# Where GpSimd clears tiles and splits weights in a four-block attention and expert kernel

## Chip, cores and metric

The kernel runs on one core of one Trainium2 chip. The metric is the device time of one execution in microseconds (us). The engines are TensorE (PE), VectorE (DVE), ScalarE (ACT), GpSimd (POOL) and SyncE (SP, which issues all DMAs here).

## What is computed

x has 4 images of 256 tokens of 128 values; the context has 4 images of 64 tokens. Four residual blocks follow one another:

```python
x = x + cross_attention(layernorm(x), ctx)            # 16 heads of 8, biases on q, k, v, out
x = x + moe(layernorm(x))                             # 8 experts, top 2 by sigmoid, relu squared, plus one shared
x = x + decoder(layernorm(x), ctx)                    # a: causal self-attention and norm; c: cross-attention
                                                      # and norm; f: dense, relu, norm
x = x + experts(layernorm(x))                         # top 1 of 7 by softmax, gated silu 512 wide, plus one shared
```

The result must be precise to float32, so most products are made from a high and a low half in float16 (high times high, high times low, low times high: L877 to L879). Each weight and each activation that enters such a product is first split: the high half is a cast, the low half the difference.

## The kernel before

**Work and its tiles.** The images are b = 0 to 3, in two groups g = 0 (images 0, 1) and g = 1 (images 2, 3). All the work is cut into events, each a tuple such as `("scores", a, b, u)`: attention a (0 cross-attention of the first block, 1 self-attention, 2 cross-attention of the third), image b, unit u. An attention of an image is: `nat` (the q or k product) and its `stack` (three DMAs by SP that lay the high and low halves into interleaved partitions), `kblocks` (DVE spreads the keys block-diagonally, four copies: into KBX for the context, L1431, into kbs for self-attention, L1429), `max` (PE makes scores, DVE takes the maximum of each head, L1484: 4 units, 12 in self-attention), `negmax` (the negated maxima scaled and split by DVE, L1493 and L1496, turned by PE, laid into the stacked queries by a DMA of SP), `scores` (PE, then the exponential on ACT), `pv`, `o_take`, `out_norm`, `flip` and `square` (the output product and the residual sum). `ln_stats` is DVE's mean and variance, `ln_pow` POOL's power -1/2, `ln_plain`, `ln_center` and `ln_norm` the rest of a norm. `gate0` is the first expert gate (13 small steps of DVE, L1531 to L1552), `spread` lays its weights over the partitions through the tile wpad (L1640, L1641, PE L1091), `up0` and `down0` are the experts.

**Weights.** They come in 11 pieces into the two halves of wraw (`load`, by SP). `split` (DVE, L1379) casts a piece to its high half wh; `split_low` (POOL, L849, three events a piece, 0 to 2) subtracts and writes wl. A piece may be loaded once the piece two before it has been split. Pieces 0 to 2 serve the attentions and the first experts, pieces 3 to 10 (1536 columns each) only the last block.

**Clearing.** `kbs_zero` (POOL, L827 to L831) clears kbs and VS, which self-attention needs later. KBX has been cleared at the start.

**What sets the order.** Nothing is ordered by hand. `steps()` says which event must come behind which. `parts()` gives each event its engines and their planned durations. `schedule()` is a list planner: among the events that could start soonest it takes the one with the largest urgency, which is the longest planned chain behind it, less GROUP_LEAD for group 1, plus numbers of the table PRESSING by kind, group and name. Its result is one fixed order per engine; each engine then runs its list in that order and waits on semaphores. Where the planner leaves PE idle, `keep_running` puts filling matmuls on the identity matrix (L888), as many as the planned gap asks for.

```python
def urgency(e):
    return todo[e] - GROUP_LEAD * group(e) + PRESSING.get(e[0], 0) + PRESSING.get((e[0], group(e)), 0) + ...
```

POOL's two branches that matter here, as they were:

```python
elif kind == "kbs_zero":
    for i in range(2):
        nc.gpsimd.memset(kbs[:, i].bitcast(U32), 0).then_inc(zeroed, 1)
...
elif kind == "split_low":
    _, i, j = e
    pool.wait_ge(w_high, nth[("split", i)])
```

Of the kernel before, what the change touches and what calls it, by code (L numbers as in the profile page):

```python
# [16 lines left out]
B, S, SC = 4, 256, 64  # L17
# [36 lines left out]
GROUP_LEAD = 5.7  # L54
TABLE_LOAD = 1.3
FLIGHT = {"load": 4.3, "stack": 2.0, "clear": 3.5, "negmax": 2.0, "fetch": 3.0, "slots": 3.0}
# [9 lines left out]
def steps():  # L66
# [3 lines left out]
    def chain(seq, *first):  # L70

        prev = list(first)
        for e in seq:
            after.setdefault(e, []).extend(prev)
            prev = [e]
        return prev[0]

    def also(e, *before):
        after[e].extend(before)

    bias = chain([("bias",)])
    ctx = chain([("split", 0), ("ctx",)])
    k0 = chain([("kblocks", 0, 0)], chain([("stack", "k0", 0)], chain([("nat", "k0", 0)], ctx, bias)))
    masks1 = chain([("masks1",)])
    biases = chain([("bias_split",)], ("split", 1))
    room = chain([("kbs_zero",)], *[("ln_pow", "x0", b) for b in range(B)])
    v0 = chain([("vctx", 0)], k0)
    for i in range(1, PIECES):
        if i >= 2:
            chain([("load", i)], ("split_low", i - 2, 2) if i > 2 else ("split", 0), *([("load", i - 1)] if i > 2 else []))  # L90
        chain([("split", i)], ("split", i - 1), *([v0] if i == 1 else [("load", i)]))
        chain([("split_low", i, j) for j in range(3)], ("split", i), *([("split_low", i - 1, 2)] if i > 1 else []))

    k2 = chain([("stack", "k2", 0)], chain([("nat", "k2", 0)], ("split_low", 2, 2), k0, ("up0", 0, 5, 0)))
    k2 = chain([("kblocks", 2, 0)], k2, *[("scores", 0, b, 3) for b in range(B)])
    chain([("slots",)], chain([("vctx", 2)], ("split_low", 2, 2), ("up0", 0, 5, 0)), ("nat", "k2", 0))

    def stack(name, b, *first):
# [105 lines left out]
    for g in range(G):  # L204
        both = (2 * g, 2 * g + 1)
        turned = []
        for b in both:
            chain([("bo_add", b)])
            e = normed("x0", b)
# [15 lines left out]
        for b in both:  # L225
# [3 lines left out]
            e = ln("f", b, chain([("square", "f", b)], e))  # L229
            also(("ln_norm", "f", b), ("b3_add", b))  # L230
            turned.append(normed("x3", b, e))
        experts1(g, [("ln_plain", "x3", b) for b in both], turned)
    return after


# [31 lines left out]
def parts(e):  # L267

    k = e[0]
# [196 lines left out]
def build(nc, x, ctx, const, weights, down0, qkbias, rows, gates, places, fill, outer, out):  # L466
# [26 lines left out]
    with ExitStack() as stk:  # L493
# [299 lines left out]
        def _(pool):  # L793
# [19 lines left out]
            for e in orders["pool"]:  # L813
# [11 lines left out]
                elif kind == "kbs_zero":  # L825
                    for i in range(2):
                        nc.gpsimd.memset(kbs[:, i].bitcast(U32), 0).then_inc(zeroed, 1)  # L827
# [929 lines left out]
```

## Time and profile before

| | |
|---|---|
| three runs | 301.47, 305.37, 304.11 us, median 304.11 |
| profiled execution | 306.42 us, span of its instructions 304.1 us |
| busy in the span | PE 259.9 us (85%), DVE 229.9 (76%), ACT 160.3 (53%), POOL 121.2 (40%) |
| mean granted PE clock | 0.949 |
| chain that ended last | PE 61%, DVE 22%, issue 6%, ACT 4%, POOL 3%, DMA 2% |

In the rows, `out<-in` are the tiles written and read, `ps` is PSUM. A timeline row is: start in us, duration in us, engine, line, operation, tiles, count, and in brackets how long the engine had stood idle and what released it. A row of stretches is: start:end, length, then busy time and count of PE, PEld (weight loads), DVE, ACT and POOL, the granted PE clock as a share of the full one, the DMA share and GB/s. A row of waits is: who waited for whom, total us, times, longest. L numbers are lines of the kernel before.

### The profile page before, as it was taken

What the parts mean: (1) busy time and instruction counts of PE and PEld (TensorE: products, weight loads), DVE (VectorE), ACT (ScalarE), POOL (GpSimd) and SP (SyncE); (2) the same over time, 40 slices, a digit from 0 to 9 for tenths busy, and PEclk for the clock granted to TensorE, in tenths of its full rate; (3) what the DMA queues carried; (4) which work ended last, traced back from release to release, by engine and by line L of the source; (5) the groups of instructions that cost most, each with busy time, mean ns of one, the idle gap of its engine ahead of it and who ended that gap; (6) DMA issues with size and microseconds to landing.
All of it is one profiled execution on the core that took longest, in us unless ns stands there. A gap on an engine that the chain in (4) does not pass through costs nothing.

```text
span 304.1 us, 7265 instructions
## 1 busy us (share of the span) xinstructions
PE 259.9 (85%) x2625; PEld 190.0 (62%) x2625; DVE 229.9 (76%) x652; ACT 160.3 (53%) x358; POOL 121.2 (40%) x172
## 2 busy tenths in 40 slices
PE   4627895879988796999999989786799999999995
PEld 4525364456856553575566566555438999659994
DVE  4688949857796989835998885978686898893572
ACT  2520464618647503386457567353666678536660
POOL 5891246946449705000100021314127566244651
PEclk9986999759999978899999999999879999999999
DMA  7930070333712400120010101010013011050121
GB/s 200 331 92 12 6 228 34 114 104 106 235 62 62 147 17 0 54 57 13 2 37 2 39 4 39 2 28 2 0 72 138 2 47 62 3 205 6 59 83 34
DMA packets 16761, 20.84 MB, mean 69 GB/s; under 512 B 1908, under 2 KB 13304, under 8 KB 16728
## 3 DMA queue, kind: packets, MB, share of 16 engines
q1 hardware_dynamic: 16728, 20.40, 20.7%
q8 instruction: 21, 0.34, 0.5%
q14 instruction: 12, 0.10, 0.1%
HBM read 11.41 MB, written 0.52 MB: 39 GB/s over the span
## 4 chain that ended last, share of the span: by engine, by line
PE 61%; DVE 22%; issue 6%; ACT 4%; POOL 3%; DMA 2%; SPq 0%; DVEq 0%; ACTq 0%; POOLq 0%
PE ps L877 8%; PE ps L878 7%; PE ps L879 7%; PE ps L1116 4%; PE ps L1061 4%; DVE MX L1484 3%; PE ps L1179 3%; DVE KBX L1431 3%; PE ps L1031 3%; PE ps L1003 2%; PE ps L1033 2%; PE ps L1052 2%; PE ps L1209 2%; PE ps L965 2%; PE ps L1000 2%
## 5 line engine op out<-in xcount | busy, mean ns | idle before, releaser
L1484 DVE TENSOR_REDUCE MX<-ps 128x8 f32<-128x512 f32 (+2 forms) x80 | 51.3, 682 | 8.1 <-PE ps L1003 4.4
L1266 ACT ACTIVATE room<-ps 128x384 f32<-128x384 f32 (+1 forms) x96 | 44.2, 534 | 12.6 <-PE ps L1033 4.9
L818 POOL TENSOR_SCALAR rstd<-mv 128x2 f32<-128x2 f32 x28 | 7.9, 282 | 105.9 <-DVE mv L1446 105.0
L701 POOL TENSOR_TENSOR room<-room 128x512 f16<-128x512 f32 x28 | 32.8, 1176 | 42.5 <-ACT room L1310 42.4
L849 POOL TENSOR_TENSOR wl<-wraw,wh 128x512 f16<-128x512 f32 (+2 forms) x30 | 33.3, 1137 | 21.6 <-DVE wh L1379 21.6
L888 PE MATMUL ps<-cst 128*128 128x128 f32 x134 | 22.9, 303 | 5.5 <-DMA cst<-in_const 4.1
L1661 DVE TENSOR_TENSOR room<-ps,hr 128x512 f32<-128x512 f32 x28 | 19.0, 682 | 10.2 <-ACT hr L1304 8.8
L1304 ACT ACTIVATE hr<-ps 128x512 f32<-128x512 f32 x28 | 16.7, 597 | 17.7 <-PE ps L879 16.0
L888 PEld LDWEIGHTS ps<-cst 128*128 128x128 f32 x134 | 19.0, 209 | 8.7 <-DMA cst<-in_const 4.1
L1310 ACT CAST room<-room 128x512 f16<-128x512 f32 x28 | 17.2, 618 | 8.1 <-DVE room L1661 7.5
L877 PE MATMUL ps<-tH,wh 128*128 128x512 f16 (+1 forms) x50 | 19.4, 389 | 1.5 <-DVE tL L1411 1.2
L1116 PE MATMUL ps<-wd,room 128*128 128x128 f32 x144 | 19.4, 283 | 0.0
L878 PE MATMUL ps<-tL,wh 128*128 128x512 f16 (+1 forms) x50 | 19.4, 388 | 0.0
L1116 PEld LDWEIGHTS ps<-wd,room 128*128 128x128 f32 x144 | 18.6, 200 | 1.1
L878 PE MATMUL ps<-xs,wh 128*128 128x128 f16 x112 | 19.2, 219 | 0.0
L877 PE MATMUL ps<-xs,wh 128*128 128x128 f16 x112 | 19.2, 219 | 0.0
L879 PE MATMUL ps<-xs,wl 128*128 128x128 f16 x112 | 19.2, 219 | 0.0
L879 PE MATMUL ps<-tH,wl 128*128 128x512 f16 (+1 forms) x50 | 19.0, 380 | 0.0
L1648 DVE TENSOR_TENSOR room<-hr,ps 128x512 f32<-128x512 f32 x16 | 10.8, 683 | 9.2 <-ACT hr L1298 7.6
L1031 PE MATMUL ps<-QS,kbs 128*128 128x256 f16 x64 | 17.6, 275 | 0.1
L1033 PE MATMUL ps<-trib,identb 128*128 128x256 bf16 x64 | 17.4, 272 | 0.0
L877 PE MATMUL ps<-wh,room 128*128 128x128 f16 x88 | 15.6, 219 | 1.5 <-POOL room L701 1.5
(231 smaller groups left out, 753.8 us busy)
## 6 DMA issues: line engine op xcount, KB each, us to landing
wraw<-in_weights SPq DMA_DIRECT2D x8, 768.0 KB, 4.3
wraw<-wh SPq DMA_DIRECT2D x6, 384.0 KB, 2.6
wraw<-wl SPq DMA_DIRECT2D x6, 384.0 KB, 3.0
QS<-tH SPq DMA_DIRECT2D x24, 64.0 KB, 2.0
QS<-tL SPq DMA_DIRECT2D x12, 64.0 KB, 2.0
hr<-xs SPq DMA_DIRECT2D x12, 64.0 KB, 2.2
rowb<-in_rows SPq DMA_DIRECT2D x1, 708.0 KB, 4.4
wraw<-in_weights SPq DMA_DIRECT2D x1, 576.0 KB, 6.4
```

Of the source, the lines that this page charges most:

```text
L701: return engine.tensor_tensor(hlo[:, g, k % NPV, :], hh[:, g, k % 2, :], hhi[:, g, k % NPV, :], ALU.subtract)
L849: nc.gpsimd.tensor_tensor(wl[:, cols], wraw[:, i % 2, first:end], wh[:, cols], ALU.subtract).then_inc(w_ready, 1)
L877: nc.tensor.matmul(o, a[0], b[0], start=start, stop=False, **kw)
L878: nc.tensor.matmul(o, a[0], b[1], start=False, stop=False, **kw)
L879: return nc.tensor.matmul(o, a[1], b[0], start=False, stop=stop, **kw)
L888: nc.tensor.matmul(ps[b][:, 0:P], ident, consts("tri_q", P), start=True, stop=True)
L1031: nc.tensor.matmul(o[:, 0:S], kb[:, j, h, 0:P], QS[:, g, j, q0:q0 + S], start=True, stop=True)
L1033: mm = nc.tensor.matmul(o[:].rearrange("p (c k) -> p c k", k=S)[:, :, 0:P], identb[:], trib[:, 1, :].unsqueeze(1).broadcast_to([P, 2, P]), ...
L1116: mm = nc.tensor.matmul(o[:, tt], hid0[g][k % NPV][:, tt], w, start=(k == 0 and t == 0), stop=(k == E0 - 1), skip_group_check=True)
L1266: nc.scalar.activation(probabilities(a, b, u), src[:, 0:width], ACT.Exp, scale=SCALE[a]).then_inc(pr_ready, 1)
L1484: nc.vector.tensor_reduce(o, v, AX_X, ALU.max).then_inc(max_read, 1)
L1661: nc.vector.tensor_tensor(hh[:, g, k % 2, :], src[:], hr[:, g, k % 2, :], ALU.mult).then_inc(hid_ready[1], 1)
```

## The change

Two waits are added on POOL, with the dependences that tell the planner of them. The clearing `kbs_zero` now waits until the context keys are spread (`kblocks 0 0`), and the first low half of piece 3 (LATE = 3) waits until the keys of image 1's self-attention are spread (`kblocks 1 1`, the second of group 0); all later low halves are behind it on POOL's list, and with two halves of wraw the loads and casts from piece 5 on can't run ahead of it either. GROUP_LEAD goes from 5.7 to 10.5, several planned durations change, and the table PRESSING has new numbers throughout, so the order on every engine is new. What each event computes is unchanged.

```diff
-GROUP_LEAD = 5.7
+GROUP_LEAD = 10.5
+LATE = 3
...
-PRESSING = {'add0': 1074, 'add1': 2092, 'b3_add': -11, 'back': -104, ...
+PRESSING = {'add0': -29, 'add1': 416, 'b3_add': 1237, 'back': -486, ...
...
-    room = chain([("kbs_zero",)], *[("ln_pow", "x0", b) for b in range(B)])
+    room = chain([("kbs_zero",)], *[("ln_pow", "x0", b) for b in range(B)], k0)
...
+    also(("split_low", LATE, 0), ("kblocks", 1, 1))
     return after
...
-            ... "rank": [("pe", .35), ("dve", 2.9)],
+            ... "rank": [("pe", .35), ("dve", 3.3)],
-            ... "bias_split": [("dve", 1.6)], ...
+            ... "bias_split": [("dve", 2.0)], ...
-            "gate0": [("pe", 1.), ("dve", 4.0)], "gate1": [("pe", .9), ("dve", 3.5)],
-            "ctx": [("pe", .9), ("act", .4), ("dve", 2.4)], "vctx": [("pe", .7), ("dve", .9)], ...
-            ... "ln_pow": [("pool", 1.95 if e[1:2] in (("x0",), ("x1",), ("x2",), ("x3",)) else 1.36)], ...
+            "gate0": [("pe", 1.), ("dve", 3.75)], "gate1": [("pe", .9), ("dve", 3.1)],
+            "ctx": [("pe", .9), ("act", .4), ("dve", 1.0)], "vctx": [("pe", 1.2), ("dve", .9)], ...
+            ... "ln_pow": [("pool", 1.6 if e[1:2] in (("x0",), ("x1",), ("x2",), ("x3",)) else 1.05)], ...
...
                 elif kind == "kbs_zero":
+                    pool.wait_ge(kb_ready, nth[("kblocks", 0, 0)])
                     for i in range(2):
...
                 elif kind == "split_low":
                     _, i, j = e
                     pool.wait_ge(w_high, nth[("split", i)])
+                    if (i, j) == (LATE, 0):
+                        pool.wait_ge(kb_ready, nth[("kblocks", 1, 1)])
```

**DVE, ahead of the key product.** The rows are DVE's list behind the cast of piece 0: `stat` and `mv` belong to `ln_stats`, `room<-hr,cst` to the bias, `copies` to the context. Before:

```order
L1443 BN_STATS stat<-X 128x6 x2
L1446 BN_AGGR mv<-stat 128x2 x2
L1443 BN_STATS stat<-X 128x6 x2
L1446 BN_AGGR mv<-stat 128x2 x2
L1364 TENSOR_SCALAR room<-hr,cst 128x2x128
L1365 SCALAR_TENSOR_TENSOR room<-hr,cst,room 128x2x128
L1385 TENSOR_TENSOR copies<-ps,copies 128x256
L1388 COPY copies<-copies 128x512 x2
```

The same place now:

```order
L1448 BN_STATS stat<-X 128x6 x2
L1451 BN_AGGR mv<-stat 128x2 x2
L1448 BN_STATS stat<-X 128x6 x2
L1451 BN_AGGR mv<-stat 128x2 x2
L1448 BN_STATS stat<-X 128x6 x2
L1451 BN_AGGR mv<-stat 128x2 x2
L1448 BN_STATS stat<-X 128x6 x2
L1451 BN_AGGR mv<-stat 128x2 x2
L1390 TENSOR_TENSOR copies<-ps,copies 128x256
L1393 COPY copies<-copies 128x512 x2
L1369 TENSOR_SCALAR room<-hr,cst 128x2x128
L1370 SCALAR_TENSOR_TENSOR room<-hr,cst,room 128x2x128
```

The statistics of images 2 and 3 have moved ahead of context and bias, and the context ahead of the bias.

**POOL, from the third `ln_pow` of the second block on.** `wl<-wraw,wh` are low halves, L837 is `b3_add`. Before, behind the low halves of piece 2:

```order
L849 TENSOR_TENSOR wl<-wraw,wh 128x512 [waits w_high] x11
L818 TENSOR_SCALAR rstd<-mv 128x2 [waits ln_stat]
L822 TENSOR_SCALAR shift<-mv 128x2 [waits pool_step]
L823 TENSOR_TENSOR rstd<-rstd,neghalf 128x2 [waits pool_step]
L824 TENSOR_TENSOR shift<-shift,rstd 128x2 [waits pool_step]
L849 TENSOR_TENSOR wl<-wraw,wh 128x512 [waits w_high] x4
```

Now, from the second `b3_add` on, which is behind the norms of the third block of images 0 and 1:

```order
L840 TENSOR_TENSOR X<-X,rowb 128x256 [waits plain_done,in_small]
L854 TENSOR_TENSOR wl<-wraw,wh 128x512 [waits kb_ready,w_high]
L820 TENSOR_SCALAR rstd<-mv 128x2 [waits ln_stat]
L824 TENSOR_SCALAR shift<-mv 128x2 [waits pool_step]
L825 TENSOR_TENSOR rstd<-rstd,neghalf 128x2 [waits pool_step]
L826 TENSOR_TENSOR shift<-shift,rstd 128x2 [waits pool_step]
L854 TENSOR_TENSOR wl<-wraw,wh 128x512 [waits w_high]
L840 TENSOR_TENSOR X<-X,rowb 128x256 [waits plain_done,in_small]
L854 TENSOR_TENSOR wl<-wraw,wh 128x512 [waits w_high] x4
```

Eleven low halves stood right behind the third norm of the second block; the first of them is now behind the norms of the third block and waits for kb_ready, the semaphore of the spreadings.

**DVE, around the first self-attention.** `kbs<-hr` are spreadings, MX maxima, MP `negmax`, `wh<-wraw` casts of pieces. Before, around the spreading of image 0:

```order
L1379 CAST wh<-wraw 128x1536
L1648 TENSOR_TENSOR room<-hr,ps 128x512
L1429 COPY kbs<-hr 32x4x256 x4
L1648 TENSOR_TENSOR room<-hr,ps 128x512 x2
L1484 TENSOR_REDUCE MX<-ps 128x4 x4
```

Now, around the spreading of image 2:

```order
L1448 BN_STATS stat<-X 128x6 x2
L1451 BN_AGGR mv<-stat 128x2 x2
L1384 CAST wh<-wraw 128x1536
L1489 TENSOR_REDUCE MX<-ps 128x2 x3
L1434 COPY kbs<-hr 32x4x256 x4
L1498 TENSOR_SCALAR MP<-MX 128x4x4 x2
L1501 SCALAR_TENSOR_TENSOR MP<-MP,MX 128x4x4 x2
```

The last of the eleven casts used to stand ahead of image 0's spreading; now piece 5's, the sixth, stands ahead of image 2's, and five more come behind it, among the maxima and norms of images 1 to 3.

## Rows read from the trace of the kernel before

**Rows 1.** Stretches of the run: start:end, us, busy time of each engine, granted clock, DMA.
```profile
17.00:25.00 8.00, 1.52 (x13) 1.22 (x12) 7.67 (x6) 0.74 (x3) 6.66 (x6) 0.75 0.15 43
56.00:72.00 16.00, 12.64 (x71) 7.97 (x69) 11.49 (x24) 7.66 (x14) 8.96 (x9) 0.71 0.48 153
104.00:130.00 26.00, 20.75 (x132) 12.46 (x131) 23.72 (x50) 6.02 (x21) 5.81 (x12) 0.87 0.10 28
120.00:200.00 80.00, 75.49 (x761) 48.08 (x761) 62.15 (x177) 47.38 (x119) 9.52 (x20) 0.98 0.08 24
```

**Rows 2.** PE's waits from 18 to 60, the chain, and the DVE and POOL timelines there.
```profile
PE ps L986 <- DVE KBX L1431: 6.5, 1, 6.5
...
17.26 5.33 DVE KBX L1431
...
17.26 7.18 DVE L1431 COPY KBX<-K 32x1024 f16<-32x1024 f16 x4 [0.48 <-DMA K<-KN]
...
16.79 3.57 POOL L827 MEMSET kbs<- 128x2048 uint32 x2
20.28 2.03 POOL L828 MEMSET VS<- 128x2304 f32 x1
```

**Rows 3.** Timeline of DVE at three spreadings, and of POOL beside the second.
```profile
90.46 1.71 DVE L1431 COPY KBX<-K 32x1024 f16<-32x1024 f16 x4
102.03 4.03 DVE L1429 COPY kbs<-hr 32x1024 f16<-32x1024 f16 x4
118.22 1.70 DVE L1429 COPY kbs<-hr 32x1024 f16<-32x1024 f16 x4
...
101.59 3.75 POOL L849 TENSOR_TENSOR wl<-wraw,wh 128x512 f16<-128x512 f32 x3 [0.97 <-DVE wh L1379]
```

**Rows 4.** POOL's timeline at the first gate; DVE's busy time in both gates, L1540 to L1545.
```profile
52.84 7.43 POOL L849 TENSOR_TENSOR wl<-wraw,wh 128x512 f16<-128x512 f32 x6
...
55.95:60.33 4.38, 4.27 (x5) 0.71 0.54 168
83.05:83.84 0.79, 0.67 (x4) 1.00 0.98 395
```

**Rows 5.** DVE's and PE's timelines ahead of the key product.
```profile
6.73 0.48 DVE L1443 BATCH_NORM_STATS2 stat<-X 128x6 f32<-128x128 f32 x2
8.29 0.33 DVE L1364 TENSOR_SCALAR room<-hr,cst 128x256 f16<-128x256 f32 x1
9.05 0.42 DVE L1385 TENSOR_TENSOR copies<-ps,copies 128x256 f16<-128x256 f32 x1
9.50 0.49 DVE L1388 COPY copies<-copies 128x512 f16<-128x512 f16 x2
...
10.50 0.27 PE L877 MATMUL ps<-copies,wh 128*128 128x256 f16 x1
```

**Rows 6.** Groups by line (ns min/median/max, or mean), and the page's loads.
```profile
L1484 DVE TENSOR_REDUCE MX<-ps x80: 658/681/693, 25.2 to 208.5; 128x8 f32<-128x512 f32 x32, 128x2 f32<-128x512 f32 x32, 128x4 f32<-128x512 f32 x16
...
L1493 DVE TENSOR_SCALAR MP<-MX x24: 159/166/732, 29.1 to 210.1; 128x16 f16<-128x16 f32 x24
...
L1379 DVE CAST wh<-wraw 128x1536 f16<-128x1536 f32 x8 | 7.7, 967 | 0.4 <-DMA wraw<-in_weights 0.4
...
wraw<-in_weights SPq DMA_DIRECT2D x8, 768.0 KB, 4.3
```

**Rows 7.** PE's waits from 60 to 104, and its filling matmuls (L888) from 80 to 88.
```profile
PE ps L1091 <- DVE wpad L1641: 4.6, 2, 3.4
...
80.00:88.00 8.00, 1.27 (x8) 1.05 (x8) 1.00 0.53 167
```

**Rows 8.** The chain at 104, and PE's timeline ahead of the second maxima.
```profile
104.24 1.93 issue
...
114.64 2.00 PE L888 MATMUL ps<-cst 128*128 128x128 f32 x16
118.91 0.44 PE L933 MATMUL ps<-cst,lni 128*128 128x128 f32 x2 [2.27 <-ACT lni L1317]
```

More of the change, by code:

```diff
@@ L294, in parts @@
             "split_low": [("pool", 1.18)],
-            "lo1": [("pool", 1.17)], "xsplit": [("act", .6), ("pool", 1.2)], "rank": [("pe", .35), ("dve", 2.9)],
+            "lo1": [("pool", 1.17)], "xsplit": [("act", .6), ("pool", 1.2)], "rank": [("pe", .35), ("dve", 3.3)],
             "onehot": [("dve", 2.1)], "spill": [("dve", .9)], "sort_high": [("pe", .87), ("act", .6)], "sort_low": [("pe", .87), ("dve", .7)],
@@ L298, in parts @@
             "downr": [("pe", .67), ("act", .29), ("dve", .3)], "back": [("pe", .45)],
-            "flip": [("pe", .25), ("act", .37)], "turn": [("pe", .25), ("act", .7 if e[1:2] in (("x1",), ("x3",)) else .37), ("dve", .42)], "v1": [("pe", .34), ("act", .45)], "bias_split": [("dve", 1.6)], "square": [("pe", .5), ("dve", .42)],
+            "flip": [("pe", .25), ("act", .37)], "turn": [("pe", .25), ("act", .7 if e[1:2] in (("x1",), ("x3",)) else .37), ("dve", .42)], "v1": [("pe", .34), ("act", .45)], "bias_split": [("dve", 2.0)], "square": [("pe", .5), ("dve", .42)],
             "negmax": [("dve", .5), ("pe", .13), ("act", .37), ("sp", .65)], "load": [("sp", .35)], "clear": [("sp", .5)],
@@ L302, in parts @@
             "hi1": [("act", .62)], "add1": [("dve", 1.2 if e[2:] == (1,) else .7)], "ln_stats": [("dve", .65)],
-            "gate0": [("pe", 1.), ("dve", 4.0)], "gate1": [("pe", .9), ("dve", 3.5)],
-            "ctx": [("pe", .9), ("act", .4), ("dve", 2.4)], "vctx": [("pe", .7), ("dve", .9)], "bias": [("dve", .7)],
-            "b3_add": [("pool", .65)], "ln_pow": [("pool", 1.95 if e[1:2] in (("x0",), ("x1",), ("x2",), ("x3",)) else 1.36)], "masks1": [("act", .75)], "kbs_zero": [("pool", 6.)], "bo_add": [("pool", .65)]}[k]
+            "gate0": [("pe", 1.), ("dve", 3.75)], "gate1": [("pe", .9), ("dve", 3.1)],
+            "ctx": [("pe", .9), ("act", .4), ("dve", 1.0)], "vctx": [("pe", 1.2), ("dve", .9)], "bias": [("dve", .7)],
+            "b3_add": [("pool", .65)], "ln_pow": [("pool", 1.6 if e[1:2] in (("x0",), ("x1",), ("x2",), ("x3",)) else 1.05)], "masks1": [("act", .75)], "kbs_zero": [("pool", 6.)], "bo_add": [("pool", .65)]}[k]
 def group(e):
```

2 lines of the change are left out of this document (1 added, 1 removed).

## The prediction

> **What bounds the kernel now.** I read the stretches first, then who waits for whom, then the timelines around the largest holes. In [rows 1] TensorE (PE) is busy 75.49 of the 80 us from 120 to 200, and VectorE (DVE) 62.15 of them: that stretch is PE's, with DVE 17.85 us short of full. The holes lie ahead of it: PE is busy 1.52 us of 8 from 17 to 25, 12.64 of 16 from 56 to 72, and 20.75 of 26 from 104 to 130. In the last two the granted clock is 0.71 and 0.87, so part of them ran at the lower level of 1.2 GHz in place of 2.4, each time behind a stretch in which PE had waited. Time won ahead of 120 us is therefore won on the path, and work that is put behind 120 must fit into DVE's 17.85 us.
>
> The largest hole has one cause. The spreading of the context keys (`kblocks 0 0`, four copies to KBX) takes DVE 7.18 us from 17.26, and PE waits 6.5 us for it in one piece. Its first copy alone lasts 5.33 us, to 22.59. Meanwhile GpSimd clears: kbs from 16.79, VS from 20.28 to 22.31 [rows 2]. Four such copies with GpSimd out of the way take 1.71 us (at 90.46, the second use of KBX) or 1.70 (at 118.22, self-attention keys). At 102.03 they take 4.03 us, beside GpSimd's low halves of the weights, 101.59 to 105.34 [rows 3]. The first expert gate shows the same: its five instructions on L1540 to L1545 fill 4.27 us while GpSimd works through six low halves (52.84 to 60.27); in the second gate these lines fill 0.67 us [rows 4].
>
> The Trainium skill (SBUF — State Buffer, section "SBUF: two separate sides") says that DVE and GpSimd share a port pair as an exclusive lock, held for a whole instruction; copies and casts within SBUF take it, and so do instructions with two SBUF inputs, the latter only against GpSimd work that reads. By that rule, the trace agrees: the copy of 5.33 us ends 0.28 us after VS. The rule speaks against this change as well, since a low half meets the other spreadings and the casts where it is moved to; that is the second rival below.
>
> **Part 1: the clearing waits for the context keys.** The spreading shrinks by 7.18 - 1.71 = 5.5 us. But DVE's new order puts the statistics of images 2 and 3 and then the context ahead of the bias (first pair of order rows), and the key product needs both. Before, the bias starts at 8.29, the context at 9.05, and PE's key product at 10.50 [rows 5]. Now four statistics at (8.29 - 6.73) / 2 = 0.78 us end at 6.73 + 3.12 = 9.85; context 0.45, its copies 0.49 and bias 0.76 end at 11.55, and the product starts at 11.65, about 1.2 us later (0 to 3, by when the second half of X lands). Net -4.3. The clearing, 3.57 + 2.03 us and two small memsets [rows 2], now runs from about 20 to 26 beside the first maxima and the first `negmax`. The maxima don't suffer: 80 of them last 658 to 693 ns. But one scaling of `negmax` took 732 ns where the median is 166 [rows 6], and beside VS it could wait the whole 2.03 us. I take +1.0 (0 to 2). Behind the clearing on GpSimd stand only the low halves of piece 1, whose cast comes far later on DVE: covered. Part 1: -3.3 (-5.5 to +1).
>
> **Part 2: no piece from 3 on is worked by GpSimd before `kblocks 1 1`.** 24 low halves leave the stretch from 52 to 105 us.
> - First gate: 4.27 - 0.67 = 3.6 us [rows 4]. It is on the path: PE waits 4.6 us for wpad in two waits, the longest 3.4 [rows 7]. But ahead of this gate now stand the norm, residual sum and statistics of image 3, which came behind it: 0.78 + 3 x 0.4 = 2.0 us of DVE by [rows 5]. I put half of it on the path, +1.0. Net -2.6 (-3.6 to 0).
> - Second gate: its matmuls now come among the first half's experts, and no filling stands ahead of `spread 1`. Before, PE had the other of the two waits there, 1.2 us, and ran 1.27 us of filling [rows 7]. I take -2.0 (-2.5 to 0).
> - First self-attention spreading: 4.03 - 1.70 = 2.3 us, of which PE stood still 1.93 [rows 3, 8]. -1.9 (-2.3 to 0).
> - Hole before the second block of maxima: 2.00 us of filling and 2.27 of waiting for image 2's layer norm [rows 8]. The new order moves that norm behind `negmax 1 0`, and PE goes on with the maxima of image 1. DVE's own chain of maxima, spreading and `negmax` stays, though, and eight fillings stand there again. -2.0 (-4.3 to 0).
>
> **Part 3: what the middle must take up.** Six casts of whole pieces (5 to 10) come to DVE between 115 and 190 us; at 0.967 us each [rows 6] they are 5.8 us. The 24 low halves are 24 x 7.43 / 6 = 30 us of GpSimd [rows 4] in some 60 us. About 32 DVE instructions of the kinds that were stretched above fall into that time: 8 spreading copies, 16 of four `negmax`, 8 of two layer norms. Each copy at 102.03 lost 2.33 / 4 = 0.58 us [rows 3]. With half of them beside a low half that is 32 / 2 x 0.58 = 9.3 us, and with all of them 18.6. DVE then needs 62.2 + 5.8 + 9.3 = 77.3 us of 80: it still fits, but without slack, and `negmax` and the norms reach PE late at times. Of these 15 us I put a third on the path: +5.0 (0 to 12).
> SyncE (SP) has the loads between its stackings. Each load waits for the piece two before it, and `stack k1 2`, `negmax 1 1` and `negmax 1 2` stand behind loads. Load 5 can go once piece 3's three low halves (3.7 us) and the small GpSimd steps between them are done, some 6 us after `kblocks 1 1`; `stack k1 2` is due then, since its product comes behind the first scores. A load takes 4.3 us to land [rows 6], and DVE meets the cast of piece 5 about then. I see 1 us there, inside the +5.
>
> **Part 4: clock and the rest.** At full clock PE's work in the two slow stretches would be shorter by 12.64 x 0.29 + 20.75 x 0.13 = 6.4 us at most [rows 1]. Smaller holes should give some of it back: -1.5 (-4 to 0). The last 100 us hold the same work in nearly the same places: 0 (-3 to +3).
>
> **Sum.** -3.3 - 2.6 - 2.0 - 1.9 - 2.0 + 5.0 - 1.5 = -8.3 us. The profiled execution took 306.4 us (span 304.1, 2.3 around it), so 298.1. The median of the runs shown is 304.1, which is 0.992 of it: 295.8.
>
> **Rivals.**
> - The waits only move (302). `negmax 0 0` takes the full 2 us, the work ahead of the first gate its full 2, nothing comes of the layer-norm hole, and the middle costs 8: part 1 is -2.3, then -1.6 - 2.0 - 1.9 + 8 - 1.5 = -1.3, with the order 2 either way: 301 to 305. For it: DVE is busy 7.67 of 8 us from 17 to 25 and 23.72 of 26 from 104 to 130 [rows 1], so it has work waiting. Against: PE's two long waits are for single stretched instructions.
> - DVE becomes the bound of the middle (slower, 312). The mechanism is the shared use of SBUF by DVE and GpSimd's low halves, at the spreadings of images 2 and 3, the `negmax` and the casts. All 18.6 us and the 5.8 of casts make 86.6 us of DVE in 80; six casts that also wait 1.5 us each for loads make it 95.6. The 15.6 us over the 80 stand on the path, and half of the gains ahead of it (13.3 with the clock) are lost to PE's new waits: 304.1 + 15.6 - 6.7 = 313. It decides once DVE's busy time in the 80 us behind `kblocks 1 1` passes 80. For it: 4.03 against 1.70 us at 102. Against: the maxima, half of DVE's work, never stretch.
> - The middle hides everything (289). Part 3 costs 1 in place of 5, the clock gives 3 and the layer-norm hole 3.3: 295.8 - 4 - 1.5 - 1.3 = 289. For it: DVE's free 17.85 us.
> - The wait does nothing (304), if the clearing never met the copies. [Rows 2] show that it did: 2 in 100.
>
> **How the numbers follow.** Forecast 0.45, own range 292 to 300; middle hides all 0.18; waits move 0.27; no effect 0.02; DVE bound 0.08. A measurement of this kernel can tell about 2% from no change, 6 us: faster is below 298.0, slower above 310.2. Faster gets three quarters of the forecast (0.34), the hidden case (0.18) and a little of the third (0.04): 0.56. Slower gets most of the DVE case, 0.07. The rest, 0.37, is within 2%. The range runs from 288 to 304, which leaves out the DVE case and the edges.
>
> **What would show it.** Right: the four KBX copies near 1.7 us with the clearing behind them; L1540 to L1545 of the first gate near 0.7 us; the first self-attention copies at 1.7; PE's waits for wpad under 2 us. For part 3: DVE over 90% busy in the 60 us behind `kblocks 1 1`, some kbs copies above 0.6 us, PE's share there below the 94% of before. Wrong: PE or DVE waits over 1 us for loads, `negmax 0 0` holds the 2 us of VS, or the middle costs under 1 us or over 12.

## The result, and the profile after

The changed kernel takes 307.61 us (median of 4 runs, 307.21 to 309.74); the kernel before 304.16 (301.47 to 305.37). The ratio is 1.0166, with a 95% interval of 1.0112 to 1.022. Executions of the kernel before fall into faster and slower ones (300.2 to 308.4 us over all batches), and each ratio compares the fast runs of one batch. The prediction was 295.8 us in a range of 288 to 304: wrong in sign and outside its range. The profiled execution of the changed kernel took 307.21 us (span 305.0), only 0.8 more than that of before (306.4); the medians differ by 3.4. The profiled execution of before is longer than each of the four runs above, and that of the changed kernel is its shortest. The differences between traces below are measured on spans, so they show the change some 2.6 us better than the medians do.

One group of instructions divides the span in three: the adds that close the first experts (L1653, now L1658) and the second (L1671, now L1676). Before, from the trace of the kernel before; a row gives ns min/median/max, then the first and the last start.
```profile
L1653 DVE TENSOR_TENSOR X<-ps,X x2: 691/692/692, 85.5 to 114.2; 128x512 f32<-128x512 f32 x2
L1671 DVE TENSOR_TENSOR X<-ps,X x2: 691/692/692, 236.8 to 280.6; 128x512 f32<-128x512 f32 x2
```
The same two groups of the changed kernel:
```profile
L1658 DVE TENSOR_TENSOR X<-ps,X x2: 681/686/691, 80.4 to 102.7; 128x512 f32<-128x512 f32 x2
L1676 DVE TENSOR_TENSOR X<-ps,X x2: 692/692/693, 236.9 to 275.6; 128x512 f32<-128x512 f32 x2
```
The last add of the first experts now starts at 102.7 us in place of 114.2: the front is 11.5 us shorter. The first add of the second experts starts at 236.9 in place of 236.8. So the middle between them grew from 122.6 us to 134.2, by 11.6, and ate all of it. The tail to the end of the span is 67.3 us before and 68.1 after.

The front went nearly as planned. The stretches that answer to [rows 1], the fourth for the middle, and a fifth for the 60 us behind `kblocks 1 1`:
```profile
17.00:25.00 8.00, 5.12 (x45) 3.75 (x44) 7.89 (x17) 0.74 (x2) 6.30 (x6) 1.00 0.32 85
56.00:72.00 16.00, 13.89 (x81) 9.76 (x82) 9.80 (x43) 7.74 (x17) 0.00 (x0) 0.89 0.00 2
104.00:130.00 26.00, 21.01 (x196) 12.78 (x195) 22.30 (x54) 12.25 (x32) 15.09 (x19) 1.00 0.36 113
120.00:200.00 80.00, 65.55 (x644) 41.02 (x642) 69.32 (x167) 40.33 (x102) 30.72 (x37) 0.97 0.22 68
106.00:166.00 60.00, 48.20 (x463) 28.00 (x464) 54.67 (x109) 28.21 (x72) 32.13 (x35) 0.99 0.32 101
```
PE is busy 5.12 us from 17 to 25 where it was 1.52, and the granted clock is full there. But from 120 to 200 PE does 65.55 us where it did 75.49, DVE 69.32 where it did 62.15, GpSimd 30.72 where it did 9.52.

Timeline and chain of the changed kernel at the first maxima (answers to [rows 2]):
```profile
16.92 2.14 DVE L1436 COPY KBX<-K 32x1024 f16<-32x1024 f16 x4
19.12 3.55 POOL L830 MEMSET kbs<- 128x2048 uint32 x2 [1.64 <-DVE KBX L1436]
...
22.84 1.84 DVE MP L1498 x2
```
The four copies take 2.14 us (7.18 before; 1.71 undisturbed). The clearing is behind them, and its last memset (VS) now holds the scaling in `negmax 0 0`: 1.84 us for two instructions whose median was 166 ns each [rows 6]. The first gate's two selections (L1547) take 0.32 us, and the first self-attention copies 1.70 in place of 4.03 [rows 3].

The middle, DVE's timeline with the single instructions that lost time, and then the waits of PE from 104 to 200 (us in total, times, longest):
```profile
107.80 1.10 DVE L1501 SCALAR_TENSOR_TENSOR MP<-MP,MX 128x16 f16<-128x16 f16 x2
...
118.68 0.96 DVE L1384 CAST wh<-wraw 128x1536 f16<-128x1536 f32 x1 [2.03 <-DMA wraw<-in_weights]
...
122.86 2.46 DVE L1434 COPY kbs<-hr 32x1024 f16<-32x1024 f16 x4
...
134.56 2.42 DVE L1459 SCALAR_TENSOR_TENSOR lnx<-act,mv,rowb 128x128 f32<-128x128 f32 x2
137.02 2.29 DVE L1473 SCALAR_TENSOR_TENSOR lnx<-lnx,rstd,rowb 128x128 f32<-128x128 f32 x2
...
140.78 2.24 DVE L1434 COPY kbs<-hr 32x1024 f16<-32x1024 f16 x4
...
156.13 1.16 DVE L1501 SCALAR_TENSOR_TENSOR MP<-MP,MX 128x16 f16<-128x16 f16 x2
157.21 1.92 DVE L1384 CAST wh<-wraw 128x1536 f16<-128x1536 f32 x1
159.05 2.39 DVE L1459 SCALAR_TENSOR_TENSOR lnx<-act,mv,rowb 128x128 f32<-128x128 f32 x2
161.48 2.28 DVE L1473 SCALAR_TENSOR_TENSOR lnx<-lnx,rstd,rowb 128x128 f32<-128x128 f32 x2
```
```profile
PE ps L938 <- DVE lnx L1473: 8.3, 3, 4.3
PE ps L1001 <- issue: 4.0, 2, 3.1
```
Beside them GpSimd's low halves, from its timeline:
```profile
133.86 7.58 POOL L854 TENSOR_TENSOR wl<-wraw,wh 128x512 f16<-128x512 f32 x6 [1.61 <-DVE wh L1384]
...
156.01 7.60 POOL L854 TENSOR_TENSOR wl<-wraw,wh 128x512 f16<-128x512 f32 x6 [5.81 <-DVE wh L1384]
```
Six low halves in a row stand over each of these two self-attention norms, and a centering or norm of 0.34 us lasts until the low half beside it ends: 1.2 us each. The excess over the undisturbed times (0.26 for the two `MP`, 1.70 for four copies, 0.61 and 0.62 for a pair of centerings and of norms, 0.96 for a cast) adds up to 0.8 + 0.8 + 1.8 + 1.7 + 0.5 + 0.9 + 1.0 + 1.8 + 1.7 = 11.0 us on DVE. From 104 to 200 PE stands 8.3 us before the transposes of normalized tiles, in three waits; before, the same wait was 1.4.

### The profile page after: what moved, and what is told of

The parts are those of the page before. It is cut to its first block, busy times and chain, and to the rows that moved or that the text cites. A ratio compares the mean times of both kernels' runs of the same rounds, so it can differ in the third digit from the quotient of the medians.

```text
span 305.0 us, 7237 instructions
## 1 busy us (share of the span) xinstructions
PE 256.2 (84%) x2611; PEld 186.7 (61%) x2611; DVE 230.2 (75%) x652; ACT 161.0 (53%) x358; POOL 119.9 (39%) x172
## 4 chain that ended last, share of the span: by engine, by line
PE 44%; DVE 35%; issue 9%; POOL 6%; ACT 4%; DMA 1%; POOLq 0%; DVEq 0%; SPq 0%; ACTq 0%
DVE MX L1489 10%; PE ps L882 6%; PE ps L883 6%; PE ps L884 6%; PE ps L1121 4%; PE ps L1184 3%; PE ps L1066 2%; POOL rstd L825 2%; DVE stat L1448 2%; PE ps L1029 2%; PE ps L1057 2%; DVE kbs L1434 2%; DVE lnx L1459 2%; PE ps L970 2%; DVE wh L1384 2%
## 5 line engine op out<-in xcount | busy, mean ns | idle before, releaser
L1489 DVE TENSOR_REDUCE MX<-ps 128x8 f32<-128x512 f32 (+2 forms) x80 | 50.6, 684 | 6.0 <-PE ps L1008 3.7
L820 POOL TENSOR_SCALAR rstd<-mv 128x2 f32<-128x2 f32 x28 | 6.9, 245 | 86.7 <-DVE mv L1451 85.9
L893 PE MATMUL ps<-cst 128*128 128x128 f32 x120 | 21.0, 308 | 5.6 <-DMA cst<-in_const 4.2
L893 PEld LDWEIGHTS ps<-cst 128*128 128x128 f32 x120 | 17.8, 214 | 8.3 <-DMA cst<-in_const 4.2
L1259 ACT CAST MT<-ps 32x256 f16<-32x256 f32 x12 | 4.3, 361 | 31.1 <-PE ps L1016 31.0
L882 PE MATMUL ps<-tH,wh 128*128 128x512 f16 (+1 forms) x50 | 18.3, 366 | 2.3 <-ACT hr L1309 1.4
L883 PE MATMUL ps<-xs,wh 128*128 128x128 f16 x112 | 19.3, 219 | 0.0
L884 PE MATMUL ps<-xs,wl 128*128 128x128 f16 x112 | 19.3, 219 | 0.0
L882 PE MATMUL ps<-xs,wh 128*128 128x128 f16 x112 | 19.3, 219 | 0.0
L938 PE MATMUL ps<-cst,lnx 128*128 128x128 f32 x32 | 6.8, 293 | 14.3 <-DVE lnx L1473 8.3
L883 PE MATMUL ps<-tL,wh 128*128 128x512 f16 (+1 forms) x50 | 18.4, 368 | 0.0
L884 PE MATMUL ps<-tH,wl 128*128 128x512 f16 (+1 forms) x50 | 18.2, 364 | 0.0
```

Source lines behind the costliest of these rows:

```text
L882: nc.tensor.matmul(o, a[0], b[0], start=start, stop=False, **kw)
L883: nc.tensor.matmul(o, a[0], b[1], start=False, stop=False, **kw)
L884: return nc.tensor.matmul(o, a[1], b[0], start=False, stop=stop, **kw)
L893: nc.tensor.matmul(ps[b][:, 0:P], ident, consts("tri_q", P), start=True, stop=True)
L1489: nc.vector.tensor_reduce(o, v, AX_X, ALU.max).then_inc(max_read, 1)
```

## The experiments

Two names are used below: "middle" is the time from the last add of the first experts to the first add of the second, "front" what lies ahead. Each ratio is to runs of the kernel before in the same batch, with its interval; medians of different batches are compared with less certainty.

One trace a run also sets a limit. Up to `kblocks 1 1` the changed kernel and three of its variants (write-only low halves, kept off the norms, cut in four) run the same instructions, and their fronts took 102.7, 103.3, 102.0 and 102.7 us. The middle of the kernel before holds the same work in four of its variants (first wait, fine clearing with and without it, low halves in two); the five took 122.6, 122.6, 122.6, 121.0 and 120.9. A difference below some 1.6 us in one part is not told from none.

**The first wait alone.** The kernel before with one line; order and table unchanged.
```diff
                 elif kind == "kbs_zero":
+                    pool.wait_ge(kb_ready, nth[("kblocks", 0, 0)])
```


> The kernel before with only the wait of the clearing on the context keys; its order on every engine is kept. Theory 'lock' (a GpSimd instruction holds up a DVE instruction that needs the shared way into SBUF): the four KBX copies fall from 7.18 to about 1.7 us, one negmax takes up to 2 us more, and since PE waited 6.5 us for the copies in one piece, 3 to 5 us of the time go: 299 to 301 us. Rival 'absorbed' (DVE's later work takes it all up): the copies shrink as well, but the time stays within 1 us of before, 303 to 305.

Measured 297.81 us, ratio 0.984 [0.975, 0.993]: better than I expected of it. Its adds:
```profile
L1654 DVE TENSOR_TENSOR X<-ps,X x2: 677/684/691, 80.3 to 107.3; 128x512 f32<-128x512 f32 x2
L1672 DVE TENSOR_TENSOR X<-ps,X x2: 691/692/692, 229.9 to 273.7; 128x512 f32<-128x512 f32 x2
```
In these traces the front is 6.9 us shorter and the middle 122.6 as before, so nothing is given back. The ratio makes it 4.9 us. The first maxima start 5.9 us earlier (19.3 in place of 25.2), although `negmax` waits for VS here too. So the loss of the changed kernel belongs to the rest of the change, the second wait and the new table together.

**Low halves that only write.** In the changed kernel GpSimd fills each low half from piece 3 on with two memsets, 1.1 us together where the subtraction took 1.2; it leaves out the low halves of the last block's weights.
```diff
+                    if i >= LATE:
+                        nc.gpsimd.memset(wl[:, cols], 0.0).then_inc(pool_step, 1)
...
+                        nc.gpsimd.memset(wl[:, cols], 0.0).then_inc(w_ready, 1)
+                        continue
```


> The changed kernel, but each low half of pieces 3 to 10 is two memsets of wl in place of the subtraction: about 1.05 us of GpSimd that only writes SBUF, so the low halves of the last block's weights are left out. Casts, loads, their waits and the order stay. Theory 'lock', with the finer rule that an instruction of DVE with two SBUF inputs meets only GpSimd work that reads: the centering and normalizing of image 0 and 1 (2.4 and 2.3 us a pair) go back to 0.6 us a pair, while kbs copies and wh casts stay partly stretched; the time falls by 6 to 8 us to 300 to 302. Rival 'casts and loads' (the six casts and what waits for loads cost the middle): the time stays at 306 to 308. Rival 'order' (the new table is worse in the middle): also 306 to 308.

Measured 299.72 us, ratio 0.989 [0.984, 0.994]: 7.9 less than the changed kernel. PE's wait for the norms falls:
```profile
PE ps L944 <- DVE lnx L1479: 2.4, 1, 2.4
```
From 8.3 us to 2.4, with centerings at 0.34. The middle is 231.6 - 103.3 = 128.3 us. So GpSimd's reading beside DVE cost 5.9 of the 11.6, by these two traces; their spans differ by 5.3 us and the medians by 7.9. The copies of f16 are not freed by it: the spreading at 139.92 takes 2.76 us beside the memsets, none of its copies over 0.74.

**The low halves kept off the norms.** In the changed kernel:
```diff
+                    if (i, j) in ((6, 0), (8, 0)):
+                        pool.wait_ge(ln_done, nth[("ln_norm", "a", i // 2 - 3)])
```


> The changed kernel, whose low halves of piece 6 also wait for ln_norm of image 0 (attention 1) and those of piece 8 for ln_norm of image 1; the order stays. Theory 'lock': these two norms go from 4.7 to 1.2 us each, the second piece's cast and one negmax lose about 1 us of stretching each, PE's waits for lnx (8.3 us in three) fall to under 2, and the time falls by 7 to 9 us, to 299 to 301, below the kernel before. Rival 'casts and loads': the low halves only start later, loads 8 and 10 go later by up to 4 us, and the time stays at 307 or rises by 1 to 2. Rival 'order': stays within 1.5 us of 307.6.

Measured 304.36 us, ratio 1.006 [1.002, 1.010]: 3.2 gained where 7 to 9 were expected, a miss. DVE's timeline shows where the six low halves went:
```profile
134.11 0.61 DVE L1461 SCALAR_TENSOR_TENSOR lnx<-act,mv,rowb 128x128 f32<-128x128 f32 x2
134.75 0.62 DVE L1475 SCALAR_TENSOR_TENSOR lnx<-lnx,rstd,rowb 128x128 f32<-128x128 f32 x2
138.60 4.47 DVE L1436 COPY kbs<-hr 32x1024 f16<-32x1024 f16 x4
```
The norms are whole again, and the next spreading takes 4.47 in place of 2.24. The second block of six, now at 158.93, meets only one scaling (0.97 us for two, in place of 0.25). DVE is busy 109.0 us in the middle in place of 114.9, and PE's wait for the norms is 2.4 in place of 8.3, yet the middle falls only from 134.2 to 131.7. So most of what DVE and that wait gave back was not on the path.

**The low halves cut in four.** In the changed kernel, four instructions of 128 x 128 for one of 128 x 512.

> The changed kernel with each low half of pieces 3 to 10 cut into four instructions of 128 columns (about 0.3 to 0.35 us each) in place of one of 512 (1.15 us). Theory 'lock', held for one instruction at a time: DVE instructions beside them wait at most about 0.35 us, so a pair of centerings takes 1.0 to 1.3 us in place of 2.4, and the time falls by 3 to 5 us, to 303 to 305; GpSimd's total rises by some 5 us. Theory 'lock for as long as GpSimd is busy' (no gaps between its instructions are of use): centerings stay at 2.4 us a pair or grow, and so does the time, 307 to 310. Rival 'casts and loads': GpSimd's longer work delays loads, 308 to 310.

Measured 304.08 us, ratio 1.006 [1.000, 1.012], 3.5 less than the changed kernel, as the theory of one instruction had it. The centerings fall to 0.51 us on the mean, from 1.24, so such an instruction is held only until the current GpSimd instruction ends. But a low half now takes 1.7 us in place of 1.2 and its buffer comes free later. VectorE stands 3.1 us for the next load, 2.0 in the changed kernel, and PE has a wait that the changed kernel has not, for the DMA of a `negmax` that SP issues right behind a load (127.24 in place of 123.33):
```profile
DVE wh L1392 <- DMA wraw<-in_weights: 3.1, 1, 3.1
PE ps L1044 <- DMA QS<-MT: 2.4, 1, 2.4
```
The middle is 235.6 - 102.7 = 132.9 us, with PE's wait for the norms at 2.4 here too.

**The table of numbers.** First the changed kernel without its second wait and without the planner's entry for it, then the old table with both waits and both entries.
```diff
-    also(("split_low", LATE, 0), ("kblocks", 1, 1))
...
-                    if (i, j) == (LATE, 0):
-                        pool.wait_ge(kb_ready, nth[("kblocks", 1, 1)])
```


> The changed kernel with its own table of numbers and its wait of the clearing, but without the second wait: neither GpSimd's wait for the self-attention keys nor the planner's entry, so that casts and low halves may stand early again. From the first add of the experts to the first add of the second experts the kernels took 122.6 us before, 122.6 with the clearing's wait alone, 134.2 after, 128.3 with write-only low halves. Theory 'waits' (the 11.6 us come from five casts and fifteen low halves that the second wait sent into the middle): they return to the first half, the middle takes 122 to 124, and the whole is near the clearing's wait alone, 296 to 300 us; at least two norms of the middle are back at 0.34 us. Theory 'order' (the new table's order of PE and VectorE is what costs the middle): 303 us or more, with the middle at 128 or more.

> The kernel before with its own table of numbers and planner costs, but with both waits and both planner entries. Theory 'waits': the middle stretch takes 130 to 135 us as in the changed kernel, single centerings and norms of 1.1 us and more stand in it, and the whole takes 304 to 309 us. Theory 'order': the middle takes 122 to 125 and the whole 296 to 300 us, since the old table's order is kept.

Measured 329.53 us, ratio 1.085 [1.075, 1.095], and 311.52, ratio 1.026 [1.020, 1.033]. The first is the theory 'order' by its letter, but far beyond either in size: its middle is 243.9 - 102.7 = 141.2 us with the norms at 0.37 on the mean, and its tail 84.5. With the planner's entry gone the same table makes another order, and a bad one, so this run says nothing of the cost of the wait in the order of the changed kernel. The second does, with the old numbers: front 101.4, so 5.9 shorter than with the first wait alone, and middle 237.7 - 101.4 = 136.3, 13.7 longer. Against the first wait alone, the two kernels with the second wait have a front shorter by 4.6 us (new table) and 5.9 (old table) and a middle longer by 11.6 and 13.7. So the loss needs no new table; what the table itself costs or gives beside the wait was not isolated.

**Without the casts.** The kernel of the write-only low halves, in which from piece 3 on VectorE casts 64 columns of 1536 and GpSimd's two memsets clear the high and the low columns; high and low halves of the last block's weights are left out.

> The changed kernel in which, from the third weight piece on, VectorE casts 64 columns instead of 1536 and GpSimd, in place of each low half, clears the piece's high and low columns with two memsets (it leaves out high and low halves of the last block's weights). The run with write-only low halves (299.7 us) left 5.7 us of the middle's 11.6 unexplained. Theory 'casts' (each of the six casts of 0.97 us is wholly on the path, since VectorE bounds the middle): 5 to 6 us less than 299.7, so 293 to 295 us, middle 122 to 124. Theory 'order' (the left-over is from the new order or the loads): 298 to 301 us, middle 127 to 129, VectorE merely idle where the casts were.

Measured 296.97 us, ratio 0.982 [0.973, 0.991], 2.75 less than 299.72: half of what I expected. The middle is 226.9 - 101.5 = 125.4 us. The casts were worth 2.9 of their 5.8. The last 2.8 over 122.6 stay; in this run too PE waits 2.4 us for a norm that takes its full speed, and 1.4 was its longest wait for one before. The stretches of the middle, of before, the changed kernel, the write-only one and this one, show more:
```profile
114.20:236.80 122.60, 109.13 (x1054) 70.65 (x1052) 94.91 (x296) 69.76 (x164) 25.73 (x49) 0.96 0.10 30
102.70:236.90 134.20, 111.77 (x1070) 72.06 (x1069) 114.86 (x311) 71.18 (x163) 54.59 (x74) 0.96 0.19 61
103.30:231.60 128.30, 112.18 (x1070) 72.86 (x1069) 106.24 (x311) 70.71 (x163) 51.67 (x98) 0.95 0.20 64
101.50:226.90 125.40, 109.52 (x1071) 72.23 (x1070) 101.03 (x312) 70.73 (x163) 49.34 (x98) 0.97 0.21 66
```
DVE has 15 instructions more in the middle of the changed kernel, and only six are casts. Of the others, eight come from the last block, from behind the add that closed the middle, such as four routing instructions. Their group before, then in the changed kernel, with the first start in each:
```profile
L1618 DVE TENSOR_SCALAR route<-tF,cst x20: 335/344/1256, 242.7 to 292.4; 128x512 f16<-128x512 f16 x20
L1623 DVE TENSOR_SCALAR route<-tF,cst x20: 320/349/1309, 230.9 to 277.5; 128x512 f16<-128x512 f16 x20
```
So the new order also put some 4 us of DVE's other work into the middle, and the tail did not get shorter for it. That fits the 2.8 us, but no run isolates it, and 2.8 is not far above what one trace leaves uncertain.

**The clearing cut finely.** First on the kernel with the first wait alone, then on the kernel before with no wait at all.
```diff
-                        nc.gpsimd.memset(kbs[:, i].bitcast(U32), 0).then_inc(zeroed, 1)
-                    nc.gpsimd.memset(VS[:], 0.0).then_inc(zeroed, 1)
+                        for j in range(4):
+                            ins = nc.gpsimd.memset(kbs[:, i, j].bitcast(U32), 0)
+                        ins.then_inc(zeroed, 1)
+                    for g in range(2):
+                        for t in range(0, T, 2):
+                            ins = nc.gpsimd.memset(VS[:, g, t:t + 2], 0.0)
+                    ins.then_inc(zeroed, 1)
```


> The kernel before with the clearing's wait alone (297.8 us), its two memsets of kbs cut in four of 128 x 512 each and that of VS in four of 128 x 576, issued back to back. In that kernel the first scaled maxima waited 1.84 us, until the 2.02 us memset of VS ended. Theory 'released between instructions' (VectorE gets in when one GpSimd instruction ends): that pair takes at most 1.0 us, and the whole 296.5 to 297.8 us. Theory 'held until GpSimd pauses' (as the copy of 5.33 us that outlasted three memsets looks): the pair stays at 1.6 to 2.1 us, and the whole at 297.5 to 298.5 us.

> The kernel before, nothing waits, but its clearing is cut finely: eight memsets of 128 x 512 and four of 128 x 576 in place of three. With the clearing's wait the fine cut let the scaled maxima in after 0.65 us instead of 1.90. Theory 'released between instructions': the four context copies, which took 7.18 us in all (one of them 5.33), take at most 0.9 us each, 2 to 3.6 us in all; PE's hole shrinks by 3.5 to 5 us and the whole falls to 298 to 301 us, most of what the wait brings. Theory 'copies wait until GpSimd pauses' (the 5.33 us outlasted the ends of three memsets): one copy again takes 4 us or more and the whole stays at 302 to 304.5 us, so that only the wait helps.

Measured 297.20 us, ratio 0.978 [0.971, 0.985], and 305.44, ratio 1.004 [0.999, 1.010]. The groups of `negmax` scalings from 18 to 30 us, with the whole memset and with the cut one:
```profile
L1494 DVE TENSOR_SCALAR MP<-MX x5: 165/176/1899, 22.3 to 29.9; 128x16 f16<-128x16 f32 x5
```
```profile
L1499 DVE TENSOR_SCALAR MP<-MX x6: 167/173/652, 23.2 to 29.8; 128x16 f16<-128x16 f32 x6
```
The scaling gets in when one memset ends: 1899 ns became 652. The gain of 0.6 us in the medians is too small to tell from none. Without the wait, the adds, and the copies with the memsets beside them:
```profile
L1658 DVE TENSOR_TENSOR X<-ps,X x2: 681/686/691, 85.5 to 112.6; 128x512 f32<-128x512 f32 x2
L1676 DVE TENSOR_TENSOR X<-ps,X x2: 691/692/692, 233.6 to 277.4; 128x512 f32<-128x512 f32 x2
...
16.81 3.78 POOL L828 MEMSET kbs<- 128x512 uint32 x8
17.15 7.65 DVE L1436 COPY KBX<-K 32x1024 f16<-32x1024 f16 x4 [0.37 <-DMA K<-KN]
20.53 2.14 POOL L832 MEMSET VS<- 128x576 f32 x4
```
```profile
L1436 DVE COPY KBX<-K x8: 405/424/5800, 17.1 to 91.7; 32x1024 f16<-32x1024 f16 x8
```
One copy lasts 5.80 us, over the ends of all twelve memsets (0.53 and 0.58 us each), which are issued back to back. Here the copy of f16 got in only when they were done; so the fine cut did not replace the first wait, and the scaling's case does not carry over to it. It is no rule for every memset: in the write-only kernel, where GpSimd waits for a semaphore between its two memsets, no copy into kbs took more than 0.86 us. This trace is also a twin of before, with only its clearing cut: front 112.6 and middle 121.0 where before had 114.2 and 122.6. Against it the first wait alone shortened the front by 5.3 us, and the change lengthened the middle by 13.2.

**Small waits in place of the second.** The first wait, the fine clearing, and:
```diff
+                    if (i, j) == (3, 0):
+                        pool.wait_ge(g0_ready, nth[("gate0", 0)])
+                    if (i, j) == (9, 0):
+                        pool.wait_ge(kb_ready, nth[("kblocks", 1, 0)])
```


> The kernel before with the clearing's wait and the fine clearing (297.2 us), and the second wait replaced by two small ones: the low halves of weight piece 3 wait for the first gate, those of piece 9, the last three, for the first self-attention's spreading; no planner entry, the old order. Theory 'small waits keep the first half's gain' (both waits with the old table had the last add of the first experts at 101.4 us, the first wait alone at 107.3): the gate's selections fall from 2.21 and 1.08 us to 0.7 together, the spreading from 4.03 to 1.7, the middle stays at 122.6, and the whole is 293 to 296 us. Rival 'the cast pays' (the load of piece 5 can start only when piece 3's low halves are done, 5 us later): the selections are short, but the cast of piece 5 waits 2 us or more for its load, with VectorE's row behind it, and the whole is 296.5 to 299 us.

Measured 297.96 us, ratio 0.984 [0.979, 0.989]. The rival was right. The gate's selections are short (0.30 and 0.19 us, where the first wait alone had 2.21 and 1.08), but DVE's timeline also has:
```profile
54.19 0.97 DVE L1650 CAST wpad<-wt 128x32 f16<-128x32 f32 x1
55.19 1.08 DVE L1651 TENSOR_TENSOR wpad<-wt,wpad 128x32 f16<-128x32 f32 x1
56.20 1.69 DVE L1658 TENSOR_TENSOR room<-hr 128x512 f32<-128x512 f32 x1
...
61.64 0.96 DVE L1389 CAST wh<-wraw 128x1536 f16<-128x1536 f32 x1 [3.75 <-DMA wraw<-in_weights]
65.36 1.52 DVE L1389 CAST wh<-wraw 128x1536 f16<-128x1536 f32 x1 [1.44 <-DMA wraw<-in_weights]
```
The low halves start when the gate is done and hold the next three instructions, 2.7 us over their usual 0.17, 0.19 and 0.68; neither theory had seen that. And two raw buffers hold the pieces, so a late low half makes a late load and a late cast, and DVE works in order: 5.2 us of standing, a part of it in place of a wait for ACT (1.8 us there with the fine clearing alone). So the 3 us saved in the gate were spent again; PE's wait for wpad is still 2.5 us. (The trace is of an execution of 300.87 us, the longest of the six.)

**Low halves in two, in two places.** The fine clearing and each low half from piece 3 on as two instructions of 128 x 256: once on the kernel with the first wait alone, once on the changed kernel.
```diff
+                        w = (end - first) // 2
+                        for c in range(2):
...
+                            ins = nc.gpsimd.tensor_tensor(wl[:, at:at + w], wraw[:, i % 2, first + c * w:first + (c + 1) * w],
+                                                          wh[:, at:at + w], ALU.subtract)
+                        ins.then_inc(w_ready, 1)
```


> The kernel before with the clearing's wait and the fine clearing (297.2 us), each low half from piece 3 on cut in two instructions of 128 x 256, and no further wait. Theory 'released between instructions': every VectorE instruction held in the first half waits at most 0.67 us instead of 1.2, so the gate's first selections take 1.2 to 1.6 us instead of 2.21 and the spreading about 2.8 instead of 4.03; GpSimd pays 3 us more in all, beside other work; 294.5 to 297 us. Rival 'GpSimd's row is longer' (cut in four, the changed kernel's casts waited 3.1 us for loads): a cast waits over 1 us for its load and the whole is 297 to 299 us.

> The changed kernel (307.6 us) with the fine clearing and each low half from piece 3 on in two instructions of 128 x 256: the two cuts that made 294.5 us of the first wait alone. Theory 'place' (the second wait puts GpSimd's reads and the casts where VectorE has no slack, whatever the cut): the middle falls from 134.2 to 129 to 132 us, half of the 5.9 us that reads cost, the rest (casts 2.9, order 2.8) stays, and the whole is 301 to 304 us, 6 us or more behind the 294.5. Rival 'granularity' (the long hold of one instruction was the whole fault of the second wait): the whole falls to 297 us or less, since the first half keeps its 5.9 us.

Measured 294.49 us, ratio 0.975 [0.971, 0.979], and 300.66, ratio 0.989 [0.980, 0.999]. The first beats both kernels of this study: 2.5% less than before. Against the uncut low halves (297.20 us, ratio 0.978) it is 2.7 us in the medians; those are of two batches, and the intervals of the ratios overlap, so the cut itself may be worth less. Its adds, then its first self-attention spreading:
```profile
L1667 DVE TENSOR_TENSOR X<-ps,X x2: 681/686/691, 76.8 to 103.6; 128x512 f32<-128x512 f32 x2
L1685 DVE TENSOR_TENSOR X<-ps,X x2: 691/692/692, 224.5 to 268.3; 128x512 f32<-128x512 f32 x2
```
```profile
94.03 2.95 DVE L1443 COPY kbs<-hr 32x1024 f16<-32x1024 f16 x4
```
The spreading is at 2.95 (4.03 before) with low halves still beside it, the front is 103.6 (105.8 with the fine clearing alone), and the casts wait 1.0 us in all for loads. With the same two cuts the changed kernel has a front of 99.6 and a middle of 229.9 - 99.6 = 130.3 us: 4.0 less in front and 9.4 more in the middle than the first (120.9). That is near the theory 'place' and far from 'granularity': with the grain halved on both sides, the second wait and its table still lose.

## Why the prediction was wrong

- **What bounds the kernel.** Right in the front, and the long holes were causes as named. Wrong in its use for the middle: "work that is put behind 120 must fit into DVE's 17.85 us" treats DVE's idle time as a store that can be spent anywhere. Much of it lay where DVE had nothing to do, while each norm and spreading had PE behind it at once.
- **Part 1** (-3.3, bounds -5.5 to +1; from its own terms the upper one is -0.5). Direction right, size too small: the first wait alone gave 4.9 us by its ratio and shortened the front by 5.3 against the twin of before, 6.9 against the trace of before. The copies gave 5.5, as said (7.18 to 1.72). The 1.2 us for the new order of the statistics did not come: in the changed kernel the copies start at 16.92, where they started at 17.26. `negmax` lost 1.7, at the upper end, and it cost little, since the first maxima still started 5.4 us earlier. The further 1.0 us in the trace of the first wait alone is within what two traces of one order differ by.
- **Part 2** (-8.5). Too large: 11.5 - 6.9 = 4.6 us with the new table, 5.9 with the old one, each to some 1.5 us. The gate, the wpad waits and the spreading came out as forecast, single values included, but not each of their microseconds was on the path. I take it that four terms, each read from a hole, were added as if no other work set the time between them; no run shows it term by term. That the front came near is in part luck, for the two errors cancel: parts 1 and 2 and the clock made 13.3, the trace shows 11.5.
- **Part 3** (+5.0, "a third on the path", bounds 0 to 12) is the step that failed: it measured +11.6. The work that arrives was well estimated, 9.3 us of stretching where the trace has 11.0 and 5.8 of casts, with one load wait of 2.0 where I saw 1. The share on the path was not. By the runs, 5.9 us come from GpSimd's reading, 2.9 from the casts: 8.8 of 16.8, half in place of a third. The two runs took only 13.8 us off DVE's busy time in the middle (114.86 to 106.24 to 101.03), and of that it is nearly two thirds. Another 2.8 us are in neither; the prediction had no term for them. The unit was off as well: 0.58 us per instruction is the mean of four copies beside three low halves; a centering or norm under a row of six loses 0.9.
- **Part 4** (-1.5). The clock's gain in the front is inside the 11.5 and can't be told apart there, and the tail is 0.8 longer. "The same work in nearly the same places" did not hold for the last 100 us: eight instructions of DVE went from the tail into the middle.
- **The rule of the Trainium skill on the port pair** (SBUF — State Buffer, "SBUF: two separate sides") held in its telling points: two-input instructions were held by the subtraction (1.2 us) and not by the write-only filling (0.34 us). It says that the lock lasts one instruction. The runs agree for centerings and scalings; the 5.80 us of one copy over twelve memsets does not fit, nor does the 5.33 us over three that I had taken for agreement, and the measurement decides. I had cited the rule and still priced what it speaks against at a third.
- **The rivals.** "DVE becomes the bound of the middle" (8 in 100) was the nearest: DVE is busy 54.67 of the 60 us behind `kblocks 1 1`, 91%, PE 48.20, 80%, where it had 94% from 120 to 200. Its price of 312 to 313 was too high, since DVE never passed 80 us in 80; its point of decision was wrong. The loss needs no full engine. Held instructions with PE right behind them are a part of it, and not the whole: three variants brought PE's wait for the norms from 8.3 us to 2.4, and the middle fell by 5.9, 2.5 and 1.3.
- **The list of what would show it** read well: the copies, the gate, the wpad waits came; so did over 90% of DVE; and the middle of 11.6 lay just under the "over 12" that was to prove it wrong (13.2 against the twin is over it). Two signs of being wrong came outright: a load wait over 1 us (2.0), and `negmax 0 0` held by VS (1.84).

The sum by measured terms: -6.9 - 4.6 + 11.6 + 0.8 = +0.9 us, the difference of the spans. The forecast was -8.3: of the 9.2 us between them 6.6 are part 3, 1.8 the front with its clock, 0.8 the tail.

What stays open: the 2.8 us of the middle that neither reading nor casts explain, and what the new table costs or gives by itself. That the medians differ by 3.4 us where the profiled executions differ by 0.8 is in the choice of execution: 306.42 us is 2.3 above the median of before, 307.21 is 0.4 below that of the changed kernel.

## What to carry to other kernels

Before a helper engine's work is moved out of the way of one stage, list the instructions that it will meet in the other, and what waits directly for each; idle time of an engine is no place to put work unless the idle time lies where the work will. If the held engine gets in between instructions, try to cut the helper's instructions in two before moving them: here that kept the order and gave up to 2.7 us over the fine clearing, where the second wait with the new table lost 9.8 over the first wait alone. A cut or a delay also lengthens the way to the buffer's release, and the next load pays: the small waits lost up to 5.2 us of DVE's time to it, and the four pieces made a load wait of 3.1 us out of one of 2.0. And take a second trace of an unchanged stretch before a difference of 1 or 2 us is given a cause.

## What the runs showed of the hardware

- A two-input f32 instruction on VectorE of 0.34 us lasts 1.2 us beside GpSimd's subtraction of 128x512 (1.23 us each on the mean), 0.51 on the mean for the centerings with pieces of 128x128, and 0.34 beside GpSimd's memsets. The 80 maxima, reductions from PSUM, took 657 to 695 ns in every run, so none was held.
- A scaling f32 to f16 within SBUF was held by one memset (1899 ns) and got in between short ones (652 ns). A copy f16 to f16 did not: 5.80 us over twelve memsets back to back. It did where GpSimd waited for a semaphore between memsets of 0.53 us (0.86 us at most). Between subtractions such copies do get in (four in 4.03 us beside three low halves [rows 3]), though beside pieces of 0.42 us one still lasted 1.41.
- The subtraction cut in four took 0.42 us a piece against 1.2 for the whole, cut in two 0.73: some 0.15 to 0.25 us more for each further instruction.
